# Part of the first two heads' score maxima moved between the last six chunks of the projection, and the first eight heads' rows split earlier

## What is computed

```
qkv  = x @ w_qkv + b_qkv                     # 16 heads of 16, 4 sequences: 64 (b, head) pairs
q, k = rope of the last 1369 tokens: t*cos + rotate_half(t)*sin
attn = softmax(q @ k.T * 0.25);  out = attn @ v
x    = layernorm(x + out @ w_proj + b_proj)
x    = layernorm(x + ffn(x))                 # gate, up, down; both factors of every product
                                             # first rounded to 4-bit floats by blocks of 16
```

## Time and profile before

| | us |
|---|---|
| median of 3 runs | 3466.4 |
| lowest, highest | 3463.58, 3471.58 |
| the profiled execution | 3468.84 |
| its span, first to last instruction | 3466.9 |
| mean granted PE clock | 0.983 |
| PE busy, of the span | 3373.9 (97%) |
| DVE busy | 3219.7 (93%) |
| ACT busy | 2652.9 (77%) |
| POOL busy | 811.9 (23%) |

### The profile page before, as it was taken

How to read it: one execution, slowest core, us unless ns; L and a number is a source line. 1 busy time by engine, 2 the same in 40 slices (tenths; PEclk the granted TensorE clock), 3 DMA queues, 4 the chain that set the end, 5 groups by cost and what they waited for, 6 DMA issues and landing times.

```text
span 3466.9 us, 69292 instructions
## 1 busy us (share of the span) xinstructions
PE 3373.9 (97%) x27752; PEld 1516.5 (44%) x27752; DVE 3219.7 (93%) x3525; ACT 2652.9 (77%) x4946; POOL 811.9 (23%) x1045
## 2 busy tenths in 40 slices
PE   8989999999999999999999999999999999999998
PEld 4543333333333333333333333333333346677775
DVE  6778999999999999999999999999999949999997
ACT  5626888888888888888888888888888874444444
POOL 5830210101111001101010110011000016766665
PEclk9978999999999999999999999999999999999999
DMA  4531222222222122211122221122111112211110
GB/s 147 180 121 63 103 91 85 95 84 104 73 85 77 66 79 104 73 55 70 64 82 82 85 89 54 61 83 78 62 61 67 50 40 66 78 50 42 42 36 22
DMA packets 132973, 264.19 MB, mean 76 GB/s; under 512 B 30022, under 2 KB 84518, under 8 KB 114214
## 3 DMA queue, kind: packets, MB, share of 16 engines
q1 hardware_dynamic: 119520, 243.25, 19.9%
q10 hardware_dynamic: 13132, 16.52, 1.5%
HBM read 173.11 MB, written 84.93 MB: 74 GB/s over the span
## 4 chain that ended last, share of the span: by engine, by line
PE 83%; DVE 6%; ACT 4%; POOL 3%; issue 2%; DMA 1%; SPq 0%; ACTq 0%; POOLq 0%; DVEq 0%
PE ps L677 37%; PE ps L730 33%; PE ps L814 6%; PE ps L826 3%; ACT arena L941 2%; PE ps L740 1%; PE ps L717 1%; PE ps L648 1%; ACT arena L916 1%; POOL arena L1273 1%; PE ps L804 1%; DVE arena L1082 1%; POOL arena L1282 0%; DVE arena L1166 0%; DMA arena<-in_xT 0%
## 5 line engine op out<-in xcount | busy, mean ns | idle before, releaser
L1082 DVE TENSOR_REDUCE arena<-ps 128x1 f32<-128x1024 f32 x2048 | 2495.3, 1222 | 61.0 <-PE ps L677 44.9
L941 ACT ACTIVATE arena<-ps 128x512 f32<-128x512 f32 x4096 | 2222.0, 597 | 321.5 <-PE ps L717 236.5
L677 PE MATMUL ps<-kst,qst 48*128 48x512 f32 x4096 | 1518.9, 452 | 14.3 <-DVE arena L1082 12.3
L717 PE MATMUL ps<-qst,kst 51*128 51x512 f32 x4096 | 1497.8, 448 | 0.2
L730 PE MATMUL ps<-arena 128*32 128x256 f32 x16384 | 1309.9, 392 | 16.8 <-ACT arena L916 15.9
L677 PEld LDWEIGHTS ps<-kst,qst 48*128 48x128 f32 x4096 | 613.7, 188 | 871.9 <-DVE arena L1082 700.4
L730 PEld LDWEIGHTS ps<-arena 128*32 128x32 f32 x16384 | 326.3, 108 | 740.3 <-issue 409.0
L717 PEld LDWEIGHTS ps<-qst,kst 51*128 51x128 f32 x4096 | 608.4, 185 | 15.5 <-ACT arena L941 11.4
L1337 POOL TENSOR_TENSOR arena<-arena,ones 128x16 bf16<-128x16 f32 x64 | 14.2, 222 | 2305.1 <-DVE arena L1087 2305.1
L926 ACT ACTIVATE arena<-arena 128x256 f32<-128x256 f32 x64 | 32.7, 511 | 216.5 <-DVE arena L1179 216.5
L814 PE MATMUL ps<-wgT,arena 128*128 128x352 f32 x512 | 193.5, 460 | 0.3 <-DVE v_all L1232 0.3
(11 more groups left out here) (104 smaller groups left out, 2095.3 us busy)
## 6 DMA issues: line engine op xcount, KB each, us to landing
qk_parts<-arena SPq DMA_DIRECT2D x32, 1024.0 KB, 5.6
kst<-qk_parts SPq DMA_DIRECT2D x127, 256.0 KB
qst<-qk_parts SPq DMA_DIRECT2D x127, 256.0 KB
qk_whole<-arena SPq DMA_DIRECT2D x16, 1024.0 KB, 5.0
arena<-qk_whole SPq DMA_DIRECT2D x16, 1024.0 KB, 5.0
kst<-qk_parts SPq DMA_DIRECT2D x127, 128.0 KB
qst<-qk_parts SPq DMA_DIRECT2D x127, 128.0 KB
att<-arena SPq DMA_DIRECT2D x256, 34.0 KB
```

The source lines that it names most:

```text
L677: mm = nc.tensor.matmul(ps[:, i % S_BANKS, :], q[SROW:SROW + STACK, qt * P:(qt + 1) * P], k[SROW:SROW + STACK, kc * CHUNK:(kc + 1) * CHUNK ...
L717: nc.tensor.matmul(ps[:, bank_of_t(g.c, i), :], kst[g.u % 2][first:first + ROWS, kb * P:(kb + 1) * P], qst[g.u % 2][first:first + ROWS, qb ...
L941: nc.scalar.activation(pt[kb % 2][:, qb * CHUNK:(qb + 1) * CHUNK], ps[:, bank_of_t(g.c, i), :], ACT.Exp).then_inc(p_ready, 1)
L1082: nc.vector.tensor_reduce(mx[g.u % 2][:, i // 2, i % 2:i % 2 + 1], ps[:, bank:bank + 2, :].rearrange("p b t -> p (b t)"), AX.X, ALU.max).t ...
```

## The change

- FIRST_SPLIT is 3 instead of 4. SP loads the first group at step 3, stores its split and loads the second at step 4, stores that at step 6, waits until both are stored and itself issues head 0's `load_s`; head 1's follows at step 9, head 0's `load_t` at step 11. POOL splits both pieces of a group in one step, 5 and 6.
- From chunk 10 on, six score pairs go into each chunk: PE puts one (two tiles) behind each of the four q and k groups and the two v groups, in banks 6 and 7 alone, each waiting for the reduction of the pair before. These are EARLY = 36 pairs, 32 of head 0 and 4 of head 1. DVE reduces pairs 0 to 2 of a chunk before `rope` of the chunk before, pairs 3 to 5 between it and `times_cos`.
- `rope` of chunk 15 moves behind the tenth pair of head 1, POOL's `times_sin` of chunk 15 behind head 0's `split_maxima` and constants that wait for the last v group; SP's store of chunk 15 behind `load_maxima(0)`. The bias addition moves to step 8 on DVE.
- The lead-in keeps tiles 8 to 19 of head 1, with `m_tile(0)` behind tile 11. Parts of the arena are laid out in another order; ACT waits for the stores of chunks 13 and 14 before head 0, SP for all stores before the first job.

```diff
@@ -95,7 +95,7 @@
 PIECES = 2
-FIRST_SPLIT = 4
+FIRST_SPLIT = 3
 SPLIT_AT = (2, 5)
@@ -105,6 +105,13 @@
...
+SLOTS, EARLY_FROM = 6, 10
+EARLY = SLOTS * (NCH - EARLY_FROM)
+BIAS_AT, LAST_ROPE = 8, 9
@@ -176,6 +183,11 @@
...
+def s_bank(g, i):
+    return 6 + i % 2 if g.c * PAIRS + i // 2 < EARLY else i % S_BANKS
@@ -256,8 +268,11 @@
...
         qx = [take(4 * CHUNK, "p (m t) -> p m t", m=4) for _ in range(3)]
+        qx = [qx[2], qx[0], qx[1]]
         rot = [take(4 * CHUNK, "p (m t) -> p m t", m=4) for _ in range(2)]
+        rot = [rot[1], rot[0]]
@@ -290,12 +305,12 @@
...
         pt = [take(N) for _ in range(2)]
+        at_r = [take(CT * P, "p (c t) -> p c t", c=CT) for _ in range(4)]
+        jobs = [take(2 * CHUNK) for _ in range(JOB_BUFS)]
         vs = [take(KT * 32, "p (t d) -> p t d", t=KT) for _ in range(2)]
...
-        at_r = [take(CT * P, "p (c t) -> p c t", c=CT) for _ in range(4)]
-        jobs = [take(2 * CHUNK) for _ in range(JOB_BUFS)]
         xr_r = [take(C) for _ in range(4)]
@@ -439,18 +454,18 @@
...
                     load_whole(0, 0)
-                if n.c == FIRST_SPLIT + 2:
+                if n.c == FIRST_SPLIT + 1:
                     store_split(0, 0)
+                    load_whole(0, 1)
                 if n.c == FIRST_SPLIT + 3:
-                    load_whole(0, 1)
-                if n.c == FIRST_SPLIT + 5:
                     store_split(0, 1)
-            run_straight(NCH, [(0, store_parts), (0, split_first)])
-            load_t(0, 0)
-            load_s(0, 1)
-            wait_stores(sp, NCH)
+                    sp.wait_ge(split_out, 16 * PARTS * 2)
+                    load_s(0, 0)
+                if n.c == FIRST_SPLIT + 6:
+                    load_s(0, 1)
+                if n.c == FIRST_SPLIT + 8:
+                    load_t(0, 0)
+            run_straight(NCH - 1, [(0, store_parts), (0, split_first)])
@@ -466,6 +481,7 @@
...
             load_maxima(0)
+            store_parts(At(0, NCH - 1))
@@ -549,6 +565,8 @@
...
                 if g in JOB_AT:
+                    if g == JOB_AT[0]:
+                        wait_stores(sp, NCH)
                     load_job(JOB_AT.index(g))
@@ -648,6 +666,7 @@
...
                     mm.then_inc(qk_psum, 1)
+                    early_pair(n, m)
                 if n.static(0):
@@ -658,26 +677,39 @@
...
-            run_straight(NCH, [(0, project), (2, weights)])
-            pe.wait_ge(qk_out, 4 * NCH)
-            pe.wait_ge(prep, 6)
+                    early_pair(n, 4 + v)
+            def early_pair(n, slot):
+                k = SLOTS * (n.c - EARLY_FROM) + slot
+                if k >= 0:
+                    for i in range(2):
+                        s_tile(At(0, k // PAIRS), 2 * (k % PAIRS) + i)
...
                 pair = i // 2
+                k = g.c * PAIRS + pair
                 if i == 0:
                     pe.wait_ge(s_in[g.u % 2], g.quad(128, 64 * (g.u // 2 + 1)))
-                if i % 2 == 0 and not (g.static(0) and pair < 2):
-                    pe.wait_ge(s_done, g.times(PAIRS, pair - 1))
+                if i % 2 == 0 and k == 0:
+                    pe.wait_ge(prep, 6)
+                    pe.wait_ge(bias_done, 1)
+                elif i % 2 == 0 and k < EARLY:
+                    pe.wait_ge(s_done, k)
+                elif i % 2 == 0 and k >= EARLY + 2:
+                    pe.wait_ge(s_done, k - 1)
                 qt, kc = i // CHUNKS, i % CHUNKS
                 q, k = qst[g.u % 2], kst[g.u % 2]
-                mm = nc.tensor.matmul(ps[:, i % S_BANKS, :], q[SROW:SROW + STACK, qt * P:(qt + 1) * P],
+                mm = nc.tensor.matmul(ps[:, s_bank(g, i), :], q[SROW:SROW + STACK, qt * P:(qt + 1) * P],
                                       k[SROW:SROW + STACK, kc * CHUNK:(kc + 1) * CHUNK], start=True, stop=True)
...
+            run_straight(NCH, [(0, project), (2, weights)])
+            pe.wait_ge(qk_out, 4 * NCH)
@@ -778,15 +810,13 @@
...
-            for i in range(TILES_S):
-                s_tile(At(0, 0), i)
-            for i in range(AHEAD):
+            first = 2 * (EARLY - PAIRS)
+            for i in range(first, AHEAD):
                 s_tile(At(0, 1), i)
-                if i == 7:
+                if i == first + 3:
+                    pe.wait_ge(v_out, 2 * NCH)
                     m_tile(0)
             pe.wait_ge(b_const, 2)
-            pe.wait_ge(v_out, 2 * NCH)
-            pe.wait_ge(bias_done, 1)
             each_head(head)
@@ -888,13 +918,7 @@
...
-            def first_rows(n):
-                if n.static(FIRST_SPLIT + 8):
-                    act.wait_ge(split_out, 16 * PARTS * 2)
-                    load_rows_of(act, SROW, 0, 0, 0, s_in[0])
-            run_straight(NCH, [(0, qk_out_of_psum), (2, weights_out), (2, first_rows)])
+            run_straight(NCH, [(0, qk_out_of_psum), (2, weights_out)])
             act.wait_ge(v_psum, 2 * NCH)
@@ -954,6 +978,9 @@
...
+            for p in (1, 2):
+                act.wait_ge(parts_out[p], 16 * (NCH // 3))
             each_head(head)
@@ -1067,24 +1094,36 @@
...
-            run_straight(NCH, [(1, rope), (0, times_cos), (0, later_weights)])
-            dve.wait_ge(bias_psum, 1)
-            nc.vector.tensor_tensor(bp_bc[:, :], ps[:, 6, 0:C], bp_bc[:, :], ALU.add).then_inc(bias_done, 1)
+                if n.static(BIAS_AT):
+                    dve.wait_ge(bias_psum, 1)
+                    nc.vector.tensor_tensor(bp_bc[:, :], ps[:, 6, 0:C], bp_bc[:, :], ALU.add).then_inc(bias_done, 1)
+            def pair_of_maxima(g, i):
+                bank = s_bank(g, 2 * i)
+                dve.wait_ge(s_psum, g.times(PAIRS, i + 1))
+                nc.vector.tensor_reduce(mx[g.u % 2][:, i // 2, i % 2:i % 2 + 1],
+                                        ps[:, bank:bank + 2, :].rearrange("p b t -> p (b t)"), AX.X, ALU.max
+                                        ).then_inc(s_done, 1)
+                if i == PAIRS - 1:
+                    dve.wait_ge(s_done, g.times(PAIRS, i + 1))
+                    nc.vector.tensor_reduce(nm[g.u % 2], mx[g.u % 2], AX.X, ALU.max, negate=True).then_inc(neg_max, 1)
+            def early_pairs(n, slots):
+                for slot in slots:
+                    k = SLOTS * (n.c - EARLY_FROM) + slot
+                    if k >= 0:
+                        pair_of_maxima(At(0, k // PAIRS), k % PAIRS)
+            run_straight(NCH, [(0, lambda n: early_pairs(n, (0, 1, 2))), (1, lambda n: rope(n) if n.c < NCH - 1 else None),
+                               (0, lambda n: early_pairs(n, (3, 4, 5))), (0, times_cos), (0, later_weights)])
...
                 for i in range(PAIRS):
-                    bank = 2 * i % S_BANKS
-                    dve.wait_ge(s_psum, g.times(PAIRS, i + 1))
-                    nc.vector.tensor_reduce(mx[g.u % 2][:, i // 2, i % 2:i % 2 + 1],
-                                            ps[:, bank:bank + 2, :].rearrange("p b t -> p (b t)"), AX.X, ALU.max
-                                            ).then_inc(s_done, 1)
-                    if i == PAIRS - 1:
-                        dve.wait_ge(s_done, g.times(PAIRS, i + 1))
-                        nc.vector.tensor_reduce(nm[g.u % 2], mx[g.u % 2], AX.X, ALU.max, negate=True).then_inc(neg_max, 1)
+                    if g.c * PAIRS + i >= EARLY:
+                        pair_of_maxima(g, i)
+                    if g.c == 1 and i == LAST_ROPE:
+                        rope(At(0, NCH - 1))
                     if i == 23 and g.c >= 4:
@@ -1256,6 +1295,12 @@
...
             nc.gpsimd.memset(wu_n[LEFT:P, 5, :], 0.0).then_inc(w_pad, 1)
+            pool.wait_ge(w_pad, 1)
+            nc.gpsimd.memset(ones[:, :], 1.0)
+            for s in range(2):
+                mm = nc.gpsimd.memset(kst[s][0:MROWS, :].bitcast(F32), 1.0)
+            mm.then_inc(b_const, 1)
+            pool.wait_ge(b_const, 1)
             def round_weights(w):
@@ -1283,34 +1328,32 @@
...
                 for u in range(2):
-                    piece = n.c - FIRST_SPLIT - 3 * u - 2
-                    if 0 <= piece < PIECES:
-                        split(u, piece)
+                    if n.c == FIRST_SPLIT + 2 + u:
+                        for piece in range(PIECES):
+                            split(u, piece)
...
-            run_straight(NCH, [(0, times_sin), (0, split_first), (0, later_weights)])
-            wait_stores(pool, NCH)
-            for s in range(2):
-                mm = nc.gpsimd.memset(kst[s][0:MROWS, :].bitcast(F32), 1.0)
-            mm.then_inc(b_const, 1)
-            pool.wait_ge(b_const, 1)
-            nc.gpsimd.memset(ones[:, :], 1.0)
-            for p in range(2):
-                nc.gpsimd.memset(vs[p][:, :, DH + 1:], 0.0)
-                mm = nc.gpsimd.memset(vs[p][:, :, DH:DH + 1], 1.0)
-            mm.then_inc(b_const, 1)
-            pool.wait_ge(v_out, 2 * NCH)
-            pool.wait_ge(b_const, 2)
-            nc.gpsimd.memset(power[:, :], -0.5)
-            nc.gpsimd.memset(steady[:, :], STEADY).then_inc(b_const, 1)
```

(21 more changed lines are left out.)

## The result

The changed kernel took 3489.02 us (median of 4 runs, 3483.74 to 3490.68), before 3467.38 in the same session: ratio 1.0055, 95% interval 1.0042 to 1.0069. It is slower by 0.55%, 15 to 24 us, above the 3486 at which the forecast's range ended. The profiled execution took 3489.02 with a span of 3487.0, at a granted clock of 0.986 (0.983 before), PE busy 3372.2 us. PE's work is the same; the time is mostly idle time and slow clock ahead of the heads.

The account below looks back on a forecast made before the run. TensorE's work on 64 heads was taken as the bound. Line 717 was put at 157.0 + 5 x 17.0 + 3.4 + 24.6 = 270.0 against 268.56, so 3466.4 + 1.4 = 3467.8 us, range 3448 to 3486.

Parts of the forecast that it names:

- upstream: Before chunk 10: earlier splitting delays w_down's quantising and everything behind by 4.2 us; chunk 10 at 147.1, its predecessor's times_cos ending 157.0.
- the loop: Chunks with six pairs: instruction order through four engines, with times_cos waiting for times_sin, sets a period of 17.0 us.
- pair 0 comes at 157.4 (+0.4): Chunk 10's first pair: rows landed at 156.2, PE waiting from 148.8, DVE free at 157.0; 0.4 us late.
- wanted by PE only in chunk 11: nothing: ScalarE's first eviction of chunk 10 waits for chunk 7's store to some 155 to 160; claimed cost nothing.
- the loop's PE term: PE's part of each chunk's loop: pair 0.43 plus group 1.72 us, twice, 4.3 us in all.
- I take none for the forecast: Chunks 11 to 15: no clock loss from PE's 2.9 us idle; up to 4.3 us per chunk kept for the range.
- The end of the stage: From the end of chunk 14's times_cos to the start of line 717, the first transposed tile: 24.6 us.
- rival "clock": Idle of 2.9 us drops PE to 1.2 GHz in chunks 11 to 15, 3 us each: 15 more, 3483; chance 0.22.
- the 3 that the forecast already held for chunk 10: Slow clock after PE's 7.4 us idle in chunk 10 adds 2.2 to 4.3 us to the loop; 3 taken.
- rope of chunk 15 ... nothing: The 2.2 us rope, now inside head 0's half-clock stretch where DVE is 38% idle, costs nothing; 2.2 at full clock.
- head clock: Head 0's half-clock stretch of 25.7 us changes length: 3456 (sooner back, chance 0.14) or 3479 (longer, 0.08).
- It doesn't do what it says: Head 0's rows land some 20 us late, pairs start only in chunk 11 or 12: 3480 or more; chance 0.05.

Follow-up runs that it names:

- e2: Changed kernel with POOL's multiplication by the sines waiting for DVE's by the cosines from chunk 10 on: 3465.71 us, ratio 0.9990.
- e1: Kernel before with the earlier splitting alone, head 0's rows issued early by SyncE, no pair moved: 3484.37 us, ratio 1.0045.
- e9: Kernel before with the earlier splitting alone, head 0's rows still issued by ScalarE's queue in step 14, no pair moved: 3471.38 us, ratio 1.0006.
- e3: Changed kernel with six extra, discarded score matmuls before each chunk's second pair from chunk 10 on: 3486.06 us, ratio 1.0045.
- e14: Changed kernel with head 0's rows loaded by six transfers, eight rows outermost in the source, in place of four: 3480.73 us, ratio 1.0034.
- e10: Kernel before with only the changed end of the stage; splitting and head 0's rows as before, no pair between chunks: 3464.73 us, ratio 0.9992.
- e12: Changed kernel, pairs from chunk 12, cosines before sines, rows by ScalarE's queue in column halves, second four loads a chunk later: 3468.61 us, ratio 1.0003.

## Why the prediction was wrong

**Right: upstream.** Chunk 10 at 147.02 (said 147.1), the transposes of w_down 5.0 us later (4.2), times_cos of chunk 9 ending at 157.84 (157.0). The agreement to 0.1 us is luck: in the fifteen other kernels with the earlier splitting chunk 10 starts anywhere from 143.84 to 149.64. **Right: the loop.** DVE's cosines held behind POOL's sines set the period, not PE or DVE alone; taking that wait away (e2) made 23 us of medians.

**Failed: "pair 0 comes at 157.4 (+0.4)".** Its first reduction was at 161.75. The store of the split took 8.2 us from its first issue, not 6.2 (6.6 counted that way in the trace before), and the four loads 17.0, not 15.0. The loads had two 1 MB stores (issued at 146.35 and 151.37) and a load of x (147.22) behind them, those of the earlier trace rows one such store (196.69); that this made the 2 us wasn't tried. 4.4 us.

**Failed: the store of chunk 7, "wanted by PE only in chunk 11: nothing".** It is wanted in chunk 10, by way of ScalarE's order: the v eviction of chunk 9 stands behind the first eviction of chunk 10, and PE's v groups of chunk 10 wait for it. Alone the early rows cost 13 us by this (e1 less e9). In the changed kernel it lies beside the wait for the rows, which holds the same queue of PE: ScalarE is released at 162.79, and the v groups at 170.85 wait for nothing.

**Mis-sized: the loop's PE term.** Pair and group take 2.57 us, not 2.15; twice in the loop makes 17.0 into 17.84, and the undisturbed spacings are 17.8.

**Failed: "I take none for the forecast"**, the clock in chunks 11 to 15. The five spacings sum to 95.6 us; without dips they are 5 x 17.77 = 88.9, so dips hold 6.7: 2.0 in chunk 10, 3.1 in chunk 12, 1.6 in chunk 13. The end of the stage, 28.2 us behind times_cos of chunk 14 where 24.6 were said, holds another 3.2. The reason given, that DVE's share doesn't depend on the clock, fails because PE's work is a link of the same loop: from the second pair to the fourth PE takes 5.15 us at full clock (182.80 to 187.95) and 8.30 in chunk 12 (200.57 to 208.87), which is the whole 3.1. PE's idle was 2.0 us, less than the 2.31 that kept the full clock in the earlier trace rows. The rival "clock" had this for three of its five chunks. The rule of the Trainium skill named with it ("TensorE: Matmul & The Clock Gate", A second HAM failure mode) would slow every one of them; the trace agrees for those three. What decides a dip is open: e3 has dips with 0.42 us of idle per chunk, e2 none with 0.16, and e14, whose loop has the same 2.0 us, has its longer spacings in other chunks (17.8, 19.4, 17.8, 20.7 and 21.0 us).

Against 270.0, then: +4.4 for the rows, +4.0 for the loop, +6.7 for dips and +3.6 for the end, less the 3 that the forecast already held for chunk 10: 285.7, measured 285.69. The 17.1 us of shift become 20.1 by the rope, below, and 2 us spread over the heads.

**Failed: "rope of chunk 15 ... nothing".** PE stood 1.92 to 2.11 us for it in every kernel that has it behind that pair, and head 1's negated maximum moved by 18.1, a us more than the first tile. That SP's later loads cost nothing held in the changed kernel, though not in e10 and e14, where PE stands 3.17 and 1.83 us for rows; and the cover is real: five pairs later cost 16 us.

**Not so:** "head clock": the half-clock stretch stayed at 25.7 us. "It doesn't do what it says": rows were 4 us late, not 20.

## What to carry to other kernels

When a step is put between others on queues that are already tight, price it by who stands behind each waiting instruction on its engine, two engines along: here a store that only one buffer wanted held TensorE through an eviction order. Let the engine with the longer chain behind it take a shared resource first (one wait on POOL was worth 23 us here). A load of few rows can be slow in itself: look at the DMA share in its tail, and put the larger dimension outermost in its source (the rows came 6.7 us sooner here, though the kernel gained 0.2% at most).

## What was not expected of the hardware

- Row loads of 0.79 MB end with a DMA share of 0.25, four of 16 engines at 25 GB/s each, and what stands behind them ends at 0.11, about two; the same bytes with eight rows outermost landed 6.7 us sooner.
- A 1 MB store queued behind such loads needs 13 to 16 us, whichever queue issues them, and a 512 KB load 21.8 in e12, against medians of 4.4 and 3.8 in the changed kernel.
- A score pair put between the groups of the projection costs PE 0.85 to 0.93 us, twice the 0.43 by itself (six tiles take 1.66 us at 272.18). The reason is open; the score tiles are in the rounded format and the groups in plain float32, and no run changed that.
- DVE's 2.28 us product takes 4.13 when it meets POOL's, and POOL's, started first, keeps its 4.53. With DVE's begun first it is POOL's that grows, to 6.60, and DVE's keeps its 2.29; with POOL's held until DVE's is through (e2) both keep their length. The Trainium skill ("SBUF — State Buffer", SBUF: two separate sides) describes the port pair of the two engines as a lock that whichever instruction starts first holds to its end; the trace agrees.
